# Transposed words side by side, and loads of the adjacency and of x over all 128 partitions

## What is computed

```python
h = jnp.maximum(_layernorm(x, axis=-1), 0.0)
Wh = h @ W_w + W_b                                  # 8192 x 256
e = leaky_relu((Wh @ a1)[:, None] + (Wh @ a2)[None, :], negative_slope=0.2)
attention = softmax(where(adj > 0, e, -9e15), axis=1)
out = x + attention @ Wh
```

## Time and profile before

| | |
|---|---|
| median of 3 runs | 1708.55 us (1708.17 to 1711.51) |
| the profiled execution | 1702.24 us |
| its span, first to last instruction | 1700.3 us |
| TensorE busy | 1524.6 us (90%) |
| ScalarE busy | 1495.0 us (88%) |
| VectorE busy | 1466.7 us (86%) |
| transfers | 300.61 MB, mean 177 GB/s |

### The profile page before, as it was taken

One profiled execution on the slowest core, in us unless ns is written; L12 is line 12 of the kernel. 1 busy time (PEld: TensorE's weight loads), 2 busy tenths in 40 slices (PEclk: granted clock), 3 DMA queues, 4 the chain that ended last, 5 costly groups with the idle time before them and its releaser, 6 DMA issues.

```text
span 1700.3 us, 30391 instructions
## 1 busy us (share of the span) xinstructions
PE 1524.6 (90%) x12228; PEld 1299.2 (76%) x12228; DVE 1466.7 (86%) x1155; ACT 1495.0 (88%) x1223; POOL 43.9 (3%) x72
## 2 busy tenths in 40 slices
PE   3851989989998999989998999989998999989998
PEld 2741877768887888878887788878887888868887
DVE  4644999999999899999999899998999899998995
ACT  3666999999999899999999899998999999998983
POOL 0530000000000000000000000000000000000000
PEclk9985999999999999999999999999999999999999
DMA  9519989769988898879989899889988898979910
GB/s 201 111 29 205 187 176 191 161 155 215 216 185 188 180 216 190 181 168 218 205 177 196 180 205 195 177 175 219 201 178 193 179 212 183 194 162 220 190 31 26
DMA packets 167711, 300.61 MB, mean 177 GB/s; under 512 B 17936, under 2 KB 34960, under 8 KB 167056
## 3 DMA queue, kind: packets, MB, share of 16 engines
q1 hardware_dynamic: 167568, 298.55, 83.3%
HBM read 290.06 MB, written 8.42 MB: 176 GB/s over the span
## 4 chain that ended last, share of the span: by engine, by line
PE 47%; ACT 18%; DVE 17%; issue 14%; DMA 3%; SPq 1%; POOLq 0%; DVEq 0%; ACTq 0%; POOL 0%
PE acc L671 35%; ACT work L355 8%; PE acc L675 8%; DVE adj_cols L507 7%; DVE work L558 5%; ACT adj_rows L339 5%; ACT work L370 4%; DVE work L565 3%; PE acc L647 3%; DMA adj_rows<-in_adj 2%; ACT X L377 1%; DMA work<-in_x 1%; PE acc L639 1%; SPq L212 1%; DVE xr L458 1%
## 5 line engine op out<-in xcount | busy, mean ns | idle before, releaser
L671 PE MATMUL acc<-X,work 128*128 128x257 f16 x10752 | 1243.2, 275 | 69.4 <-DVE work L565 69.4
L671 PEld LDWEIGHTS acc<-X,work 128*128 128x128 f16 x10752 | 1044.2, 98 | 255.8 <-DVE work L565 84.9
L558 DVE SCALAR_TENSOR_TENSOR work<-work,sigma,adj_cols 128x2048 f32<-128x2048 f32 x256 | 595.9, 2349 | 102.3 <-ACT work L355 98.9
L565 DVE TENSOR_TENSOR work<-work 128x2048 f16<-128x2048 f32 (+1 forms) x256 | 512.0, 2018 | 29.3 <-ACT work L370 28.9
L339 ACT ACTIVATE adj_rows<-adj_rows 128x2048 fp8e5<-128x2048 int32 x256 | 480.6, 1901 | 24.2 <-DMA adj_rows<-in_adj 24.2
L370 ACT CAST work<-work 128x2048 f16<-128x2048 f32 (+1 forms) x256 | 423.8, 1676 | 74.6 <-DVE work L558 73.0
L507 DVE STREAM_TRANSPOSE adj_cols<-adj_rows 128x512 int32<-128x512 int32 x256 | 271.5, 1120 | 29.7 <-ACT adj_rows L339 26.4
L355 ACT ACTIVATE work<-q_odd,r_j 128x1024 f32<-128x1024 f32 x256 | 274.5, 1136 | 14.0 <-PE acc L675 9.6
L355 ACT ACTIVATE work<-work,r_j 128x1024 f32<-128x1024 f32 x256 | 274.3, 1135 | 12.3 <-PE acc L675 8.2
L675 PE MATMUL acc<-X,work 128*128 128x257 f32 x1024 | 245.5, 384 | 0.0
L675 PEld LDWEIGHTS acc<-X,work 128*128 128x128 f32 x1024 | 187.1, 192 | 23.2
(11 more groups left out here) (63 smaller groups left out, 106.7 us busy)
## 6 DMA issues: line engine op xcount, KB each, us to landing
adj_rows<-in_adj SPq DMA_DIRECT2D x1024, 256.0 KB, 7.2
work<-in_x SPq DMA_DIRECT2D x16, 512.0 KB, 22.1
xr<-in_x SPq DMA_DIRECT2D x16, 512.0 KB, 11.7
out<-xr SPq DMA_DIRECT2D x16, 512.0 KB, 3.3
work<-q_rows SPq DMA_DIRECT2D x4, 512.0 KB, 5.9
q_odd<-q_rows SPq DMA_DIRECT2D x4, 512.0 KB, 6.0
q_odd<-in_L_gnn_W_w SPq DMA_DIRECT2D x2, 128.0 KB, 2.2
xr<-in_L_gnn_a SPq DMA_DIRECT2D x2, 128.0 KB, 6.0
```

Source lines behind the costliest of these rows:

```text
L558: nc.vector.scalar_tensor_tensor(out=slot, in0=slot, scalar=sigma[:, 0:1], in1=edges, op0=ALU.max, op1=ALU.min).then_inc(s_M, 1)
L565: nc.vector.tensor_tensor(Et[:, at:at + n, 1, :], Wt[:, i % RING, 0:n, :], Et[:, at:at + n, 0, :], ALU.subtract).then_inc(s_E, 1)
L671: return nc.tensor.matmul(acc[:, m, 0:F1], Et[:, 2 * (k % RING) + e, 1 if n == 2 else 0, m * P:(m + 1) * P], X16[:, 2 * k + e, 1 if n == 1 ...
```

## The change

The columns inside a piece of 512 are ordered anew. Word (w, c) now holds the columns 128 w + 4 c + e, so the 32 words of a transposed block lie next to each other in `nat` and `rows8`. x is loaded in the matching order: partition 32a + c, blocks 4w to 4w + 3 of piece k. With it the transfers are cut otherwise. A load of x is one (k, w) for all 128 partitions, 4 KB to a partition, where it was one (k, a) for 32 partitions, 16 KB to each. A load of the adjacency is one q for all 128 partitions, 2 KB each, where it was one a for 32 partitions, four times 2 KB each. The numbers of transfers and their sizes stay. The q store follows the new order, in runs of 4 words instead of 16, and the load of the next q row waits for one product more.

```diff
-    x_cols = x.rearrange("(a k c y) f -> a c k (y f)", a=NQ, k=NC, c=QP)
+    x_cols = x.rearrange("(a k w c e) f -> k w a c (e f)", a=NQ, k=NC, w=CW, c=QP)
     adj_v = adj.rearrange("(s n q r) (a k j) -> s n k a r q j", n=SETS, q=SQ, r=QP, a=NQ, k=NC)
-    q_store = q_dram.ap().rearrange("s r -> (s r)").rearrange("(a k c y) -> a c k y", a=NQ, k=NC, c=QP)
+    q_store = q_dram.ap().rearrange("s r -> (s r)").rearrange("(a z c e) -> a c z e", a=NQ, z=NC * CW, c=QP)
...
-                xk = x_in[:, k * Y:(k + 1) * Y, :].rearrange("p y f -> p (y f)")
-                for q in range(NQ):
-                    sp.dma_start(xk[QP * q:QP * (q + 1)], x_cols[q, :, k]).then_inc(s_x[k], 16)
+                xk = x_in[:, k * Y:(k + 1) * Y, :].rearrange("p (w e) f -> p w (e f)", e=4)
+                for w in range(CW):
+                    sp.dma_start(xk[:, w], x_cols[k, w]).then_inc(s_x[k], 16)
...
-                for q in range(NQ):
-                    sp.dma_start(nat[QP * q:QP * (q + 1), n % NAT], adj_v[s, n % SETS, n // SETS, q]).then_inc(s_nat[n % NAT], 16)
+                for q in range(SQ):
+                    sp.dma_start(nat[:, n % NAT, q], adj_v[s, n % SETS, n // SETS, :, :, q]).then_inc(s_nat[n % NAT], 16)
...
-                sp.dma_start(q_store[q], q_j[QP * q:QP * (q + 1), :].rearrange("p (k y) -> p k y", k=NC)).then_inc(s_qst, 16)
+                sp.dma_start(q_store[q], q_j[QP * q:QP * (q + 1), :].rearrange("p (z e) -> p z e", e=4)).then_inc(s_qst, 16)
...
-                        else:
-                            sp.wait_ge(s_W, NK * s)
+                        sp.wait_ge(s_W, NK * s + 1)
...
-                act.wait_ge(s_nat[n % NAT], 16 * NQ * (n // NAT + 1))
+                act.wait_ge(s_nat[n % NAT], 16 * SQ * (n // NAT + 1))
...
-            dve.wait_ge(s_x[0], 16 * NQ)
+            dve.wait_ge(s_x[0], 16 * CW)
...
-                    dve.wait_ge(s_x[k + 1], 16 * NQ)
+                    dve.wait_ge(s_x[k + 1], 16 * CW)
...
-                                    rows8[:, n % R8].bitcast(I32).rearrange("p q (c w) -> p q w c", w=CW)).then_inc(s_T, 1)
+                                    rows8[:, n % R8].bitcast(I32).rearrange("p q (w c) -> p q w c", w=CW)).then_inc(s_T, 1)
```

## The result

The changed kernel takes 2920.03 us (median of 4 runs, 2918.12 to 2921.94) beside 1708.36 us for the kernel before on the same chips. The ratio is 1.710, with a 95% interval of 1.705 to 1.715. The forecast was 3400 us in a range from 2900 to 5400.

A forecast was written before the change was run, and what follows sets the result against it. The prediction took compute engines handing work to each other as the bound, with DMA close behind; loads on four engines would become the bound: 162 + 3100 + 67 + 60 = 3389, giving 3400 us, range 2900 to 5400.

The forecast's parts named there:

- What bounds the kernel: Whole kernel before: compute throttles the loads, but with thin slack; a load path slower by a fifth becomes the bound.
- The staked step: Loads of x and adjacency: an outermost DRAM count of 4 cuts each into shares on the same four engines.
- The sum: Whole kernel on four engines at 85.2 GB/s: 162 + 3100 + 67 + 60 = 3389, giving 3400 us.
- 252 tiles x 12.3 = 3100: Adjacency loads from the fifth tile on: 12.3 us each at four engines of 21.3 GB/s, with compute hidden behind.
- The higher estimate of 25: Rate per engine of the loads: about 25 GB/s instead of 21.3, since twelve competitors are gone.
- low end: Whole kernel at 25 GB/s per engine: a tile in 10.5 us, 2902 us in all.
- The other signs: Loads and casts: some 85 to 90 GB/s, and ScalarE's casts waiting for loads some 1700 us in all.
- The front: Start of kernel: x in by 103 us, projection ending near 130, four tiles by 152, fifth tile by 162.
- The small parts: q store in 16 B runs, at most about four times 1.5 us; longer wait before next q row, taken as nothing.
- The transpose: VectorE's transpose of neighbouring words: 587 ns instead of 1120, saving 136 us of VectorE with no effect on the end.
- Rival 1, the old pace: Loads on four engines staying at 13.4 GB/s each: 5340 us; chance 0.20 including what lies between.
- Rival 2: Loads use all 16 engines, not bound to the outermost count or four others each transfer: 1640 us; chance 0.15.

The follow-up runs named there:

- the shapes with 2, 4, 8 and 16: Program of adjacency loads alone, without attention, with these outermost DRAM counts; measured DMA shares 0.13, 0.26, 0.53 and 0.99.
- the two later edits: New word order with quadrant loads, issued 0, 2, 1, 3 (1657.24 us), then also fifth and sixth tiles issued before q's round trip: 1647.92 us.

## Why the prediction came out as it did

**What bounds the kernel.** Right. The loads had a slack of a fifth, and a cut to a quarter of the engines made them the bound from end to end.

**The staked step.** Right: the number of small packets to the digit, the DMA share of 0.26 to 0.29 (0.25 to 0.3 was named), the shapes with 2, 4, 8 and 16. That the four are the same each time on SyncE's queue, a choice between two values in the prediction, is shown by the broadcast of q above. The Trainium skill's rule in "DMA: Bandwidth & Descriptors", section "Why a DMA increments its semaphore by 16 and not by 1", agrees with all of them (shares 0.13, 0.26, 0.53 and 0.99 for outermost counts of 2, 4, 8 and 16).

**The sum.** The direction and the order of its terms held, the size of one did not. The term is *252 tiles x 12.3 = 3100*: measured were 10.44 us a tile, 2631 in all, and these 469 us are nearly the whole of the 480 between forecast and result. The other terms came out within 15 us: the fifth tile was issued at 147.75, not near 162; the tiles' stretch holds 81 us above 2631, where 67 were added for other traffic; from the end of the last cast (2860.0) to the end are 60. The size came from the 21.3 GB/s per engine, read from a store and from the broadcast of q. Loads of the adjacency run faster on an engine whether 4 work (25) or 16 (24). The higher estimate of 25 stood beside it and was the right number, but its reason, twelve competitors gone, explains only the small step from 24 to 25. It gives 2910 by the prediction's own low end, 2902 and the 8 around the span; the result lies 20 us above the range's lower bound of 2900. The other signs that were named missed with the same term: 103 GB/s against 85 to 90, and 1304 us of cast waits against some 1700.

**The front.** It ended early by 14 us, and one agreement in it is luck, as errors cancelled. x ran at 105 GB/s and was in by about 85, not 103; but the front had to wait for the first quarter of x until 28 us (15.3 us of waiting, 4.9 before) and for the second until 48 (12.4 us), so that it ended at 131 (forecast: near 130). The tiles were not the last to come, as assumed (152): they were there when the first cast began at 128.69. And from the end of these casts (136.0) to the fifth tile's issue there were 11.7 us, not 7.5; most of the difference is the q store, below.

**The small parts.** The q store in 16-byte runs: it lands in 4.2 us (1.5 before), within "about four times", and SyncE waited 5.0 us for it instead of 1.1; in the word order alone it lands in 3.9. The longer wait before the next q row cost nothing that these runs show: SyncE waits 48.0 us there in the word order alone (35.8 before), and no cast waits for a load.

**The transpose.** 587 ns were forecast from the time of a word in another operation; 689 came. A gain, but four fifths of the one forecast.

**Rival 1, the old pace.** It fell. Four engines in four quadrants, or two in two (50 GB/s for (2, 32) in 64 partitions), carry 25 GB/s each and don't hinder each other. **Rival 2** fell for SyncE and stood for GpSimd; there it took 1727 us, not the 1640 forecast for it. That the 1640 is near to what quadrant loads give with the new word order (1669, and 1648 with the two later edits) owes nothing to its mechanism.

## What to carry to other kernels

Before changing how a load is cut, write down the outermost count of both sides: a load that covers all 128 partitions but walks DRAM as (4, 32) ran on 4 of 16 engines when SyncE issued it. For SyncE's transfers the number of packets under 512 B in the page shows at once on how many engines they ran, before and after; for GpSimd's it does not, as each left 208 of them. And take the rate of an engine from transfers of the same kind and direction: 21.3 GB/s from a store and a broadcast stood against 24 to 25 for these loads.

## What the runs showed that was not expected

- The order in which quadrant loads are issued matters: 0, 2, 1, 3 instead of 0, 1, 2, 3 gave 239 GB/s instead of 226 in loads alone, and 12 us of the kernel, 8.7 of it in pauses in which TensorE waits for instructions.
- With 16 engines at work the rate depends on how the partitions are dealt among them: 226 GB/s for quadrants, 256 for (16, 8), 387 for one row step of 128, each inside its stage, the last two with 128 partitions each, all with pieces of 2 KB.
- Issuing can be slow by itself. SyncE took 67.14 us for 16 loads of x and 41.69 us for 16 adjacency loads in mid-run of the changed kernel, where 20 took 12.80 us before. It shows as SPq in the chain, not as a wait.

```profile
3.06 67.14 SPq L208 DMA_DIRECT2D work<-in_x  x16
...
599.94 41.69 SPq L212 DMA_DIRECT2D adj_rows<-in_adj  x16
```
